# A fused state-space kernel: the second image of pair i + 2 scaled on VectorE instead of GpSimd, and the first cycle's scatters placed ahead of the scaling

## The chip, the cores and the metric

The kernel runs on one core of a Trainium2 chip. The metric is the device time of one execution in microseconds, as the median of three runs. A core has five engines that work side by side, each through its own queue in its own order: TensorE (PE in the profile) for matrix products, VectorE (DVE), ScalarE (ACT), GpSimd (POOL) and SyncE (SP), which here only starts DMA transfers. They meet at semaphores: an instruction waits until a counter has reached a number, and another one raises it. Matrix products land in PSUM, everything else stands in SBUF or in DRAM.

## The reference

The input x has 16 images of 256 channels and 32 x 32 points. Two residual blocks follow each other:

```
x = x + L0(group_norm(x))     # gate: softmax; experts: relu; x * sigmoid(scale per image and channel)
x = x + L1(group_norm(x))     # below, per image, N = 1024 tokens
  xz  = silu(in_proj_w @ x + in_proj_b);  x_ssm, res, gate = split(xz, 3)
  xf  = silu(conv1d(x_ssm, 3 taps, per channel) + dw_b)
  dbc = dbc_w @ xf + dbc_b;  dt, B, C per head (2 heads, 8 states)
  xf, dt, B, C reordered along the tokens by a permutation per head
  h_t = exp(dt_t * A) * h_{t-1} + dt_t * B_t * x_t;   y_t = C_t . h_t + D * x_t
  y   = y in the old order;  y = y * silu(gate) + res
  out = silu(out_proj_w @ y + out_proj_b)
```

L0 and both norms come down to one factor and one summand per image and channel. The kernel works these out from statistics of x and applies them to x once; this is the scaling that the change is about: x becomes x * P + B per channel, in place.

## The kernel before

The 16 images are worked in eight pairs. Three buffers `xb0` to `xb2` hold the pairs in turn, pair i in buffer i mod 3; each pair has two images (b = 0, 1) of two tiles of 128 channels x 1024 tokens. A loop of eight cycles runs on every engine, and cycle i of an engine holds work of three pairs: the recurrence, the gate, the residual and the output of pair i, the scattering of pair i + 1, and the scaling, the projection and the convolution of pair i + 2. Nothing plans the order: on each engine it is the order in which the functions `cycle(i)` are written, and each instruction waits for the one in front of it on its engine.

GpSimd does three things per cycle. `scale_x(i + 2, ...)` (L443, two instructions per image, one per tile) scales the images. `scatter(i + 1)` (L462) issues 16 indirect DMAs, which write the rows of `stage` into the DRAM tensor `xt_scratch` at the places that the permutation gives. `gather(i, h)` (L476) issues eight indirect DMAs per head, which bring the rows of the result back from `yt_scratch` into `crow`. `scattered` waits until all scatters have landed. Every wait of GpSimd goes through `hold`, which waits for a semaphore and counts on. In the order before, one image is scaled ahead of the scatters and the other behind them. `scale_x` waits for `pcur_ready` in front of its loop over the images:

```
if i < NB:
    hold(scales_ready, 1)
else:
    hold(pcur_ready, i + 1)
par = i % XB
for b in images:
    hold(x_in[par][b], x_loads(i))
```

`pcur_ready` is raised by VectorE when the parameters of a pair are in `pcur`: twice before the loop, then once for each later pair by `take_params` (L1027). In cycle 0 this stands late, after the parameters of pairs 2 to 7 have been worked out; in the later cycles it is VectorE's first instruction. The scatters need the bias on the rows in `stage`, which VectorE adds early in the cycle (L1046), and they need the loads of the pair before out of `xt_scratch` to be over.

TensorE begins the projection of pair i + 2 (L1429, 16 matmuls per image) behind the last matmuls of pair i's recurrence; image 0 comes first and then image 1, and each waits for its own count of scaled images. Behind them stand 24 matmuls of the residual, the turning back of the gathered rows (L1547), and the output (L1557). ScalarE empties PSUM; its results pass through VectorE's convolution (L1040). VectorE's carried states (L1120, L1122) end the recurrence of a cycle, and the convolution follows directly behind them. VectorE's last work on an image (L1225) adds the output to x; SyncE then stores the image, and loads an image of the pair three later into the same buffer.

Of the kernel before, what the change touches and what calls it, by code (L numbers as in the profile page):

```python
# [19 lines left out]
ALU = mybir.AluOpType  # L20
# [6 lines left out]
CT = C // P  # L27
H, S = 2, 8
E, R = 8, 16
NB = 2  # L30
# [37 lines left out]
PRM_P, PRM_S, PRM_B, PRM_BIAS, PRM_W = 0, 2, 4, 6, 12  # L68
# [30 lines left out]
def build(nc, x_d, w1g_d, b1g_d, w2_d, b2_d, inw_d, inb_d, dww_d, dwb_d, dbcw_d, dbcb_d, alog_d,  # L99
          alogt_d, dpar_d, mob_d, outw_d, outb_d, const_d, out_d):  # L100
    with ExitStack() as ctx:
        def sb(name, width, dt=F32):
            return ctx.enter_context(nc.sbuf_tensor(name, [P, width], dt))

        def sem(name):
            return ctx.enter_context(nc.semaphore(name))

        def v(tensor, off, *dims, parts=P, p0=0):

            width = tensor.shape[1]  # L110
            assert off + sum(step * (count - 1) for step, count in dims) < width
            return bass.AP(tensor, p0 * width + off, [[width, parts]] + [list(d) for d in dims])
# [8 lines left out]
        XB = 3  # L121
# [27 lines left out]
        pcur = sb("pcur", XB * NB * PRM_W)  # L149
# [39 lines left out]
        x_in = [[sem(f"x_in{par}{b}") for b in range(NB)] for par in range(XB)]  # L189
# [29 lines left out]
        ranks_ready = sem("ranks_ready")  # L219
        pcur_ready = sem("pcur_ready")  # L220
        x_scaled = sem("x_scaled")
        a_full, a_drained = sem("a_full"), sem("a_drained")
        g_full, g_drained = sem("g_full"), sem("g_drained")
        e_full, e_drained = sem("e_full"), sem("e_drained")
# [48 lines left out]
        def first(i):  # L273
            return isinstance(i, int) and i == 0
# [11 lines left out]
        def x_loads(i):  # L286

            return 16 * (1 + i // XB)
# [19 lines left out]
        def x_view(par, b, ct, off=0, n=N):  # L308
            return v(xb[par], (b * CT + ct) * N + off, (1, n))
# [113 lines left out]
        def _(pool):  # L423

            def hold(semaphore, value):

                if isinstance(value, int) and value <= 0:
                    return
                pool.wait_ge(semaphore, value)
                pool.sem_inc(pool_passed, 1)  # L430

            def scale_x(i, images=range(NB)):
# [8 lines that stand above are left out]
                    params = v(pcur, (par * NB + b) * PRM_W, (1, PRM_W))  # L441
                    for ct in range(CT):
                        last = nc.gpsimd.tensor_scalar(x_view(par, b, ct), x_view(par, b, ct),  # L443
                                                       params[:, PRM_P + ct:PRM_P + ct + 1],
                                                       params[:, PRM_B + ct:PRM_B + ct + 1], ALU.mult, ALU.add)
                    last.then_inc(x_scaled, 1)

            def scatter(i):
                for nt in range(NT):

                    if nt % BIAS_TILES == 0:

                        hold(stage_ready, i * BIAS_U + 2 + nt // BIAS_TILES)
                    if nt == 0:

                        hold(dbc_rows_in, 16 * (1 + H) * i)
                        for h in range(H):
                            hold(x_rows_in[h], 16 * i)
                        hold(c_stored, 16 * i)
                    for h in range(H):  # L460
                        k = h * NT + nt
                        pool.indirect_dma_start(  # L462
                            out=xt_d.ap(), out_offset=bass.IndirectOffsetOnAxis(ap=idx[:, k:k + 1], axis=0),
                            in_=v(stage, (nt * H + h) * ROW, (1, ROW)), in_offset=None).then_inc(rows_scattered, 16)

            def scattered(i):
                hold(rows_scattered, 256 * (i + 1))
# [13 lines left out]
                    hold(y_gathered[1], 128 * (i + 1))  # L481

            def cycle(i):
                if i < PH - 2:
                    scale_x(i + 2, (0,))
                if i < PH - 1:
                    scatter(i + 1)
                if i < PH - 2:
                    scale_x(i + 2, (1,))
                if i < PH - 1:  # L490
                    scattered(i + 1)
                for h in range(H):
                    gather(i, h)
# [317 lines left out]
        def _(dve):  # L811
# [207 lines left out]
            def take_params(i):  # L1019

                if i == NB:
                    dve.wait_ge(params_ready, 1)
                if i >= XB:

                    dve.wait_ge(out_ready, (i - XB + 1) * NB * CT)
                    dve.wait_ge(e_drained, (i - XB + 1) * E_U)
                nc.vector.tensor_copy(v(pcur, i % XB * NB * PRM_W, (1, NB * PRM_W)),  # L1027
                                      v(prm, i * NB * PRM_W, (1, NB * PRM_W))).then_inc(pcur_ready, 1)

            def convolve(i, b, tiles=range(CT)):  # L1030

                for ot in tiles:
                    step = (i * NB + b) * 3
                    dst = v(xf[b], ot * N, (1, N))
                    tap = lambda k: v(xs, ot * (N + 2) + k, (1, N))
                    wt = lambda k: v(small, DWW + ot * 3 + k, (1, 1))
                    for k in (1, 2):

                        dve.wait_ge(conv_step[ot], step + k)
                        nc.vector.scalar_tensor_tensor(dst, tap(k), wt(k), dst, ALU.mult, ALU.add).then_inc(conv_step[ot], 1)  # L1040
# [187 lines left out]
            def cycle(i):  # L1228
                more, beyond = i < PH - 1, i < PH - 2
                if beyond and not first(i):  # L1230
                    take_params(i + 2)
                if first(i):
                    turned_factors(i, 0)
                    scan(i, 0, 0)
                    token_products(i, 0)

                    token_weights(i, 0)
                    weights_block(i, 0)
                    scan(i, 0, 1)
                else:  # L1240
                    scan(i, 0, 0)
                    token_weights(i, 0)
                if more:
                    add_bias(i + 1, 0, 0, NT)
                    add_bias(i + 1, 1, 0, BIAS_TILES)
                if not first(i):
                    scan(i, 0, 1)
                if more:
                    add_bias(i + 1, 1, BIAS_TILES, BIAS_TILES)
                if not first(i):  # L1250
                    weights_block(i, 0)
                carried(i, 0)
                factors(i, 1)
                if first(i):
                    rescaled(1)
                token_products(i, 1)
                scan(i, 1, 0)
                if first(i):
                    turned_factors(i, 1)
                    group_variance(1, P_SUMS2, V_VAR2)  # L1260
                    token_weights(i, 1)
                    scaled(1)
                else:
                    token_weights(i, 1)
                    turned_factors(i, 1)
                weights_block(i, 1)
                scan(i, 1, 1)
                if first(i):
                    biases(1, 0, 3 * CT, P_BIAS2, params_ready)
                    take_params(i + 2)  # L1270
                carried(i, 1)
                if beyond:
                    for b in range(NB):
                        convolve(i + 2, b)
                if more:
                    softplus(i + 1)
                for b in range(NB):
                    gated(i, 0, b)
                    add_residual(i, 0, b)
                for b in range(NB):  # L1280
                    gated(i, 1, b)
                    add_residual(i, 1, b)
                if more:
                    factors(i + 1, 0)
                output(i, i % XB, 0)
                if more:
                    turned_factors(i + 1, 0)
                    token_products(i + 1, 0)
                output(i, i % XB, 1)
# [54 lines left out]
        def _(pe):  # L1344
# [88 lines left out]
            def project(i, b, before):  # L1433

                if first(i) and b == 0:
                    pe.wait_ge(x_first, 2)
                else:
                    pe.wait_ge(x_scaled, i * NB + b)
                for k in range(4):
                    o = pj_slot(k, a_drained, i * A_U + b * 4, before)  # L1440
                    part(o, i % XB, b, 0, k // 2, k % 2).then_inc(a_full, 1)
# [275 lines left out]
```

## Time and profile before

| | |
|---|---|
| median of 3 runs | 838.59 us (837.87 to 839.11) |
| the profiled execution | 842.28 us, span 840.5 us |
| PE busy | 735.4 us, 88% |
| DVE busy | 592.7 us, 71% |
| ACT busy | 508.6 us, 61% |
| POOL busy | 354.4 us, 42% |
| chain that ended last | POOL 28%, PE 20%, DMA 19%, DVE 15%, issue 13% |

The span runs from the first instruction to the last; the execution's own time is 1.8 us longer. Busy shares are means over stages with different limits: cycle 0 and the last cycles are not like cycles 1 to 5. The chain is followed back from the last instruction, at each step to what released it; "issue" in it is time for which the profile shows no wait. The rows below have start and duration in microseconds from the span's start, and in brackets the idle time of the engine ahead of the row with what ended it.

### The profile page before, as it was taken

How to read it: one execution, taken by the hardware profiler on the slowest of the kernel's cores; microseconds unless marked ns; L12 is line 12 of the kernel's file. 1: busy time of each engine (PE TensorE's matmuls, PEld its weight loads, DVE VectorE, ACT ScalarE, POOL GpSimd, SP SyncE). 2: the span in 40 equal slices, each digit the busy share in tenths (PEclk: the TensorE clock that was granted, in tenths of full speed). 3: DMA queues.
4: the chain of work that ended last, by engine and by line, in shares of the span. 5: the costliest groups of instructions: out<-in, count | busy, mean ns of one | idle time of the engine just before them, and what ended most of it. 6: DMA issues, size and time to landing. Idle time of an engine off the chain costs nothing.

```text
span 840.5 us, 11680 instructions
## 1 busy us (share of the span) xinstructions
PE 735.4 (88%) x4190; PEld 435.9 (52%) x4190; DVE 592.7 (71%) x1097; ACT 508.6 (61%) x954; POOL 354.4 (42%) x325
## 2 busy tenths in 40 slices
PE   2599867929999999999999999999999999697976
PEld 1356556614566456545755565546654566354642
DVE  5699589624787578957894779577957786378533
ACT  5775745426764875488467756676667764544422
POOL 2295300377038711873087407760577037600330
PEclk9699857969999999999999999999999999998989
DMA  9924550248464937484747564765568434942332
GB/s 329 369 101 165 143 128 1 83 134 212 107 213 144 245 87 246 136 215 120 219 143 189 164 183 156 190 194 131 195 191 213 115 131 142 254 114 87 110 92 100
DMA packets 128539, 136.40 MB, mean 162 GB/s; under 512 B 57305, under 2 KB 107106, under 8 KB 126434
## 3 DMA queue, kind: packets, MB, share of 16 engines
q1 hardware_dynamic: 114448, 99.42, 41.3%
q0 software_dynamic: 12288, 35.80, 13.1%
q10 hardware_dynamic: 1746, 0.45, 0.3%
q8 instruction: 33, 0.54, 0.3%
q14 instruction: 24, 0.20, 0.1%
HBM read 83.08 MB, written 53.61 MB: 163 GB/s over the span
## 4 chain that ended last, share of the span: by engine, by line
POOL 28%; PE 20%; DMA 19%; DVE 15%; issue 13%; ACT 4%; SPq 0%; POOLq 0%; DVEq 0%; ACTq 0%
POOL xt_scratch L462 15%; POOL crow L476 11%; DMA out<-xb 7%; PE pj L1557 7%; PE pj L1429 5%; DMA xb<-in_x 3%; DMA crow<-yt_scratch,idx 3%; DMA xt_scratch<-stage,idx 3%; DVE xf L1040 2%; DVE rs L894 2%; PE tp L1547 2%; POOL xb L443 2%; DMA crow<-cd_scratch 1%; PE tp L1449 1%; DVE xb L1225 1%
## 5 line engine op out<-in xcount | busy, mean ns | idle before, releaser
L1429 PE MATMUL pj<-xb,inw 128*128 128x512 f32 x768 | 350.4, 608 | 21.5 <-POOL xb L443 16.0
L1429 PEld LDWEIGHTS pj<-xb,inw 128*128 128x128 f32 x768 | 144.7, 194 | 187.2 <-issue 155.9
L462 POOL DMA_INDIRECT xt_scratch<-stage,idx x128 | 152.0, 1188 | 80.9 <-issue 73.7
L476 POOL DMA_INDIRECT crow<-yt_scratch,idx x128 | 135.0, 1054 | 109.5 <-DMA yt_scratch<-rs 62.1
L443 POOL TENSOR_SCALAR xb<-xb,pcur 128x1024 f32<-128x1024 f32 x30 | 46.5, 1559 | 257.2 <-DMA xb<-in_x 170.3
L1040 DVE SCALAR_TENSOR_TENSOR xf<-xs,small,xf 128x1024 f32<-128x1024 f32 x64 | 83.9, 1322 | 76.0 <-ACT xf L634 74.5
L1557 PE MATMUL pj<-gt,outw 128*128 128x512 f32 x256 | 118.9, 596 | 0.1
L734 ACT ACTIVATE rs<-pj,small 128x512 f32<-128x512 f32 x64 | 44.2, 694 | 58.1 <-PE pj L1557 58.0
L677 ACT COPY stage<-tp 128x256 f32<-128x256 f32 x128 | 47.8, 374 | 44.9 <-PE tp L1451 42.1
L690 ACT COPY rs<-pj 128x512 f32<-128x512 f32 x64 | 33.0, 600 | 67.7 <-PE pj L1524 67.7
L703 ACT ACTIVATE gt<-pj,pcur 128x512 f32<-128x512 f32 x64 | 41.5, 687 | 46.0 <-PE pj L1429 45.9
L1449 PE MATMUL tp<-dw,xf 128*128 128x162 f32 x256 | 63.3, 331 | 4.8 <-ACT stage L678 3.9
L1557 PEld LDWEIGHTS pj<-gt,outw 128*128 128x128 f32 x256 | 46.6, 192 | 38.2 <-issue 37.4
L1225 DVE SCALAR_TENSOR_TENSOR xb<-xb,pcur,rs 128x1024 f32<-128x1024 f32 x32 | 41.0, 1284 | 35.2 <-ACT rs L734 35.2
L1449 PEld LDWEIGHTS tp<-dw,xf 128*128 128x128 f32 x256 | 46.5, 204 | 36.5 <-issue 26.8
L627 ACT ACTIVATE xs<-pj,pcur 128x512 f32<-128x512 f32 x64 | 41.7, 688 | 37.5 <-PE pj L1429 30.3
L1169 DVE TENSOR_TENSOR big<-big,crow 128x1024 f32<-128x1024 f32 x32 | 60.6, 1938 | 1.1 <-DMA crow<-cd_scratch 1.0
L1451 PE MATMUL tp<-dw,xf 128*128 128x162 f32 x256 | 59.6, 317 | 0.0
L1212 DVE TENSOR_TENSOR gt<-tp,gt 128x512 f32<-128x512 f32 x64 | 41.2, 683 | 25.9 <-PE tp L1547 25.8
L724 ACT ACTIVATE rs<-pj,pcur 128x512 f32<-128x512 f32 x56 | 36.1, 687 | 28.9 <-PE pj L1429 24.7
L1547 PE MATMUL tp<-dw,crow 128*128 128x128 f32 x256 | 36.9, 286 | 15.9 <-DMA crow<-yt_scratch,idx 13.0
L665 ACT ACTIVATE big<-sg,small 128x272 f32<-128x272 f32 x128 | 50.1, 502 | 0.2
(256 smaller groups left out, 1059.0 us busy)
## 6 DMA issues: line engine op xcount, KB each, us to landing
xb<-in_x SPq DMA_DIRECT2D x16, 1024.0 KB, 5.7
xp<-xt_scratch SPq DMA_DIRECT2D x16, 1024.0 KB, 9.6
crow<-cd_scratch SPq DMA_DIRECT2D x16, 1024.0 KB
out<-xb SPq DMA_DIRECT2D x16, 1024.0 KB, 6.4
yt_scratch<-rs SPq DMA_DIRECT2D x16, 512.0 KB, 3.6
yt_scratch<-rs SPq DMA_DIRECT2D x32, 256.0 KB, 5.4
gt<-in_x SPq DMA_DIRECT2D x4, 1024.0 KB, 12.0
big<-in_x SPq DMA_DIRECT2D x4, 1024.0 KB, 13.7
```

Of the source, the lines that this page charges most:

```text
L443: last = nc.gpsimd.tensor_scalar(x_view(par, b, ct), x_view(par, b, ct), params[:, PRM_P + ct:PRM_P + ct + 1], params[:, PRM_B + ct:PRM_B ...
L462: pool.indirect_dma_start(out=xt_d.ap(), out_offset=bass.IndirectOffsetOnAxis(ap=idx[:, k:k + 1], axis=0), in_=v(stage, (nt * H + h) * ROW ...
L476: pool.indirect_dma_start(out=v(crow, k * NB * P, (1, NB * P)), out_offset=None, in_=yt_d.ap()[0:(h + 1) * N], in_offset=bass.IndirectOffs ...
L665: last = nc.scalar.activation(v(big, s * EEW, (1, EEW)), v(sg, 0, (1, EEW)), ACT.Exp, scale=v(small, ANEG + h * S + s, (1, 1)))
L1040: nc.vector.scalar_tensor_tensor(dst, tap(k), wt(k), dst, ALU.mult, ALU.add).then_inc(conv_step[ot], 1)
L1169: nc.vector.tensor_tensor(v(big, W_OFF + b * NT * L, (Q * L, S), (L, NT), (1, L)), v(big, SEG + b * NT * L, (EEW, S), (L, NT), (1, L)), v( ...
L1225: nc.vector.scalar_tensor_tensor(x_view(par, b, ot), x_view(par, b, ot), std, v(rs, (b * CT + ot) * N, (1, N)), ALU.mult, ALU.add).then_in ...
L1429: last = nc.tensor.matmul(o[:, :], v(inw, ct * 3 * C + col + ot * P, (1, P)), x_view(par, b, ct, nt * HALF, HALF), start=(ct == 0), stop=( ...
L1449: nc.tensor.matmul(v(o, 0, (1, P + HK)), tile(0), v(dw, HK, (1, P + HK)), start=True, stop=False, skip_group_check=True)
L1451: nc.tensor.matmul(v(o, P, (1, HK + P)), tile(1), v(dw, 0, (1, HK + P)), start=False, stop=True, skip_group_check=True).then_inc(x_full, 1)
L1547: last = nc.tensor.transpose(v(o, e * P, (1, P)), v(crow, (h * NT + nq * 4 + e) * NB * P + b * P, (1, P)), const("ident"))
L1557: last = nc.tensor.matmul(o[:, :], v(outw, h * C + ot * P, (1, P)), v(gt, (b * CT + h) * N + nt * HALF, (1, HALF)), start=(h == 0), stop=( ...
```

## The change

VectorE gets a `scale_x` of its own, and in cycles 0 to 5 scales image 1 of pair i + 2 behind the carried states of the second head, with two instructions and a semaphore of its own, `x_scaled_v`. GpSimd scales image 0 alone. In cycle 0 GpSimd calls `scale_x` with an empty list ahead of the scatters and scales image 0 behind them; in the later cycles it scales image 0 ahead of the scatters, and the call behind them has the empty list. TensorE waits for image 0 of the later pairs on `x_scaled`, with new counts, and for image 1 on `x_scaled_v`.

```diff
             def cycle(i):
+
+                early = 1 if i else 0
                 if i < PH - 2:
-                    scale_x(i + 2, (0,))
+                    scale_x(i + 2, range(0, early))
                 if i < PH - 1:
                     scatter(i + 1)
                 if i < PH - 2:
-                    scale_x(i + 2, (1,))
+                    scale_x(i + 2, range(early, 1))
                 if i < PH - 1:
                     scattered(i + 1)
...
+            def scale_x(i, b):
+
+                par = i % XB
+                dve.wait_ge(pcur_ready, i + 1)
+                dve.wait_ge(x_in[par][b], x_loads(i))
+                params = v(pcur, (par * NB + b) * PRM_W, (1, PRM_W))
+                for ct in range(CT):
+                    last = nc.vector.tensor_scalar(x_view(par, b, ct), x_view(par, b, ct), params[:, PRM_P + ct:PRM_P + ct + 1],
+                                                   params[:, PRM_B + ct:PRM_B + ct + 1], ALU.mult, ALU.add)
+                last.then_inc(x_scaled_v, 1)
...
                 carried(i, 1)
                 if beyond:
+                    scale_x(i + 2, 1)
                     for b in range(NB):
                         convolve(i + 2, b)
...
                 if first(i) and b == 0:
                     pe.wait_ge(x_first, 2)
+                elif i < NB:
+                    pe.wait_ge(x_scaled, i * NB + b)
+                elif b:
+                    pe.wait_ge(x_scaled_v, i - 1)
                 else:
-                    pe.wait_ge(x_scaled, i * NB + b)
+                    pe.wait_ge(x_scaled, 2 + i)
```

GpSimd's queue in cycle 0, from the end of pair 0's scatters to the gathers, before the change (a row is an instruction with its waits; `x_in20` and `x_in21` are the loads of images 0 and 1 into buffer 2):

```order
L443 TENSOR_SCALAR xb2<-xb2,pcur 128x1024 [waits rows_scattered,pcur_ready,x_in20]
L443 TENSOR_SCALAR xb2<-xb2,pcur 128x1024
L462 DMA xt_scratch<-stage,idx 2048x290 [waits stage_ready,dbc_rows_in,x_rows_in0,x_rows_in1,c_stored]
L462 DMA xt_scratch<-stage,idx 2048x290 x7
L462 DMA xt_scratch<-stage,idx 2048x290 [waits stage_ready]
L462 DMA xt_scratch<-stage,idx 2048x290 x7
L443 TENSOR_SCALAR xb2<-xb2,pcur 128x1024 [waits pcur_ready,x_in21]
L443 TENSOR_SCALAR xb2<-xb2,pcur 128x1024
L476 DMA crow<-yt_scratch,idx 128x256 [waits rows_scattered,y_stored0,w_ready]
```

The same place of GpSimd's queue after the change (lines have moved by one):

```order
L463 DMA xt_scratch<-stage,idx 2048x290 [waits rows_scattered,pcur_ready,stage_ready,dbc_rows_in,x_rows_in0,x_rows_in1,c_stored]
L463 DMA xt_scratch<-stage,idx 2048x290 x7
L463 DMA xt_scratch<-stage,idx 2048x290 [waits stage_ready]
L463 DMA xt_scratch<-stage,idx 2048x290 x7
L444 TENSOR_SCALAR xb2<-xb2,pcur 128x1024 [waits pcur_ready,x_in20]
L444 TENSOR_SCALAR xb2<-xb2,pcur 128x1024
L477 DMA crow<-yt_scratch,idx 128x256 [waits rows_scattered,y_stored0,w_ready]
```

The scaling of image 0 has moved behind the 16 scatters, the scaling of image 1 is gone, and the first scatter now carries the wait for `pcur_ready`.

VectorE's queue in cycle 0, around the end of the carried states of the second head, after the change (`hs1` are its states, `xf0` and `xf1` the convolved images):

```order
L1030 COPY pcur<-prm 128x24 [waits params_ready]
L1134 COPY hs1<-st 128x128 [waits carry_full]
L1136 SCALAR_TENSOR_TENSOR hs1<-st,dcy,hs1 128x128 x7
L1040 TENSOR_SCALAR xb2<-xb2,pcur 128x1024 [waits x_in21,pcur_ready]
L1040 TENSOR_SCALAR xb2<-xb2,pcur 128x1024
L1054 SCALAR_TENSOR_TENSOR xf0<-xs,small,xf0 128x1024 [waits conv_step0] x2
L1054 SCALAR_TENSOR_TENSOR xf0<-xs,small,xf0 128x1024 [waits conv_step1] x2
```

Two instructions stand between the carried states and the convolution that were not there; cycles 1 to 5 have the same two at the same place.

## Rows read from the trace of the kernel before

**Rows 1.** Chain of waits in cycle 2: start, duration (us), what.
```profile
315.69 11.82 DMA out<-xb
...
360.07 4.15 DMA xt_scratch<-stage,idx
...
402.33 1.30 DVE xb L1225
```

**Rows 2.** Timeline of TensorE, cycle 0: start, duration, instruction, count [idle before <-releaser].
```profile
164.73 7.13 PE L1429 MATMUL pj<-xb,inw 128*128 128x512 f32 x16
187.81 19.79 PE L1429 MATMUL pj<-xb,inw 128*128 128x512 f32 x40 [15.95 <-POOL xb L443]
```

**Rows 3.** Windows of cycle 0: stretch, its length, busy us, PEclk, DMA share, GB/s.
```profile
164.70:172.00 7.30, 7.16 (x18) 2.97 (x16) 0.00 (x0) 7.27 (x10) 5.71 (x6) 1.00 0.70 200
...
177.00:187.80 10.80, 0.00 (x0) 0.00 (x0) 0.28 (x1) 0.00 (x0) 7.17 (x7) 0.50 0.23 83
187.80:191.10 3.30, 3.29 (x4) 1.52 (x5) 0.00 (x0) 0.00 (x0) 2.57 (x3) 0.50 0.86 108
```

**Rows 4.** Timeline of TensorE in cycle 2.
```profile
358.65 24.30 PE L1429 MATMUL pj<-xb,inw 128*128 128x512 f32 x56
...
388.96 1.09 PE L1547 MATMUL tp<-dw,crow 128*128 128x128 f32 x8 [0.82 <-DMA crow<-yt_scratch,idx]
```

**Rows 5.** Timeline of GpSimd in cycle 0.
```profile
159.66 2.37 POOL L443 TENSOR_SCALAR xb<-xb,pcur 128x1024 f32<-128x1024 f32 x2 [67.07 <-DVE pcur L1027]
162.19 1.01 POOL L462 DMA_INDIRECT xt_scratch<-stage,idx  x1 [0.16 <-issue]
...
172.35 1.92 POOL L462 DMA_INDIRECT xt_scratch<-stage,idx  x1 [0.30 <-issue]
...
180.60 0.97 POOL L462 DMA_INDIRECT xt_scratch<-stage,idx  x1 [2.48 <-issue]
...
185.40 2.36 POOL L443 TENSOR_SCALAR xb<-xb,pcur 128x1024 f32<-128x1024 f32 x2
```

**Rows 6.** Timeline of VectorE in cycle 0.
```profile
134.29 0.86 DVE L1046 TENSOR_TENSOR stage<-stage,small 128x272 f32<-128x272 f32 x3
...
159.16 0.18 DVE L1027 COPY pcur<-prm 128x24 f32<-128x24 f32 x1
...
161.69 1.89 DVE L1122 SCALAR_TENSOR_TENSOR hs<-st,dcy,hs 128x128 f32<-128x128 f32 x7
172.15 5.12 DVE L1040 SCALAR_TENSOR_TENSOR xf<-xs,small,xf 128x1024 f32<-128x1024 f32 x4 [8.57 <-ACT xf L634]
```

**Rows 7.** Timeline of GpSimd in cycle 2.
```profile
341.02 3.67 POOL L462 DMA_INDIRECT xt_scratch<-stage,idx  x1 [0.30 <-issue]
...
357.55 0.96 POOL L462 DMA_INDIRECT xt_scratch<-stage,idx  x1 [0.30 <-issue]
...
361.07 2.36 POOL L443 TENSOR_SCALAR xb<-xb,pcur 128x1024 f32<-128x1024 f32 x2
365.22 1.00 POOL L476 DMA_INDIRECT crow<-yt_scratch,idx  x1 [1.79 <-DMA xt_scratch<-stage,idx]
```

**Rows 8.** Timeline of VectorE in cycle 2.
```profile
340.00 3.84 DVE L1169 TENSOR_TENSOR big<-big,crow 128x1024 f32<-128x1024 f32 x2
...
355.61 1.89 DVE L1122 SCALAR_TENSOR_TENSOR hs<-st,dcy,hs 128x128 f32<-128x128 f32 x7
366.02 7.78 DVE L1040 SCALAR_TENSOR_TENSOR xf<-xs,small,xf 128x1024 f32<-128x1024 f32 x6 [8.52 <-ACT xf L634]
```

**Rows 9.** Timeline of VectorE in the setup.
```profile
35.61 0.81 DVE L1308 TENSOR_SCALAR xb<-xb,pcur 128x1024 f32<-128x1024 f32 x1
```

**Rows 10.** Timeline of GpSimd at the same place.
```profile
35.89 1.61 POOL L443 TENSOR_SCALAR xb<-xb,pcur 128x1024 f32<-128x1024 f32 x1 [19.58 <-DVE pcur L995]
```

**Rows 11.** Instructions on the images, 310 to 410: SyncE's loads, landing times.
```profile
L320 SPq DMA_DIRECT2D xb<-in_x x2: 379/380/380, 327.5 to 330.4; - x2
...
DMA to landing us min/median/max: 5.0/5.5/12.1
```

More of the change, by code:

```diff
@@ L221, in build @@
         x_scaled = sem("x_scaled")
+        x_scaled_v = sem("x_scaled_v")
         a_full, a_drained = sem("a_full"), sem("a_drained")
```

## The prediction

> **What bounds the kernel now.** I read the chain of waits first. In cycles 1 to 5 it runs in a ring: from the finished first image of a pair through its store, the load of a new image into the same buffer, GpSimd's scaling of it, GpSimd's 16 scatters and their landing, the 16 gathers, and TensorE's output back to VectorE. In the cycle shown the store starts at 315.69 and the next first image is finished at 403.63, so one ring takes 87.9 us [rows 1]. TensorE runs beside it with little to spare: it works without a gap from 358.65 to 382.95 [rows 4], and the turning back of the second head then waits 0.82 us for the gather. So GpSimd's queue is the bound of these five cycles, by 0.8 us, and what delays its scatters or gathers delays everything.
>
> The first cycle (cycle 0) is different. The timeline of TensorE there shows a hole: 16 matmuls of the projection of pair 2 (its first image) end at 171.86, and the other 40 (second image, then the residual) start at 187.81, after 15.95 us of waiting for GpSimd's scaling [rows 2]. The granted clock falls to 0.50 in the hole and is still there after it [rows 3]. So 40 matmuls take 19.79 us, where 56 take 24.30 in a later cycle [rows 2, 4]: at that pace 40 would take 17.36, and the fall costs 2.4 us.
>
> GpSimd's own timeline says why [rows 5]: it scales image 0 from 159.66 to 162.03, issues 16 scatters from 162.19 to 185.4, and scales image 1 from 185.40 to 187.77. It starts at 159.66 because VectorE's copy of pair 2's parameters ends at 159.34 [rows 6].
>
> **The first cycle after the change.** The scatters now stand ahead of the only scaling left on GpSimd, and VectorE scales image 1 behind the carried states. Two things follow, and the first is decided by a wait. The function that scales is still called with an empty list of images, and it waits for the parameters before it looks at the list. The program order shows that: the first scatter's wait names the parameters. So the scatters can't go at 135.2, when their last bias is added [rows 6], but only once the copy has ended at 159.34. GpSimd's first action on that wait came at 159.66 before; with the scatter's other waits in between I put the first scatter at 160.2 (159.7 to 160.5), 2.0 us earlier than before, which is all that leaving out image 0 in front gives.
>
> From there, the 16 scatters took 23.2 us before. In that stand one of 1.92 us, where a plain one takes 0.96, while a convolution ran on VectorE [rows 5, 6, 7], and an idle time of 2.48 us where 0.30 is usual and for which the profile names nothing [rows 5]. The convolution now comes later (it needs the projection): minus 1.0. VectorE's new scaling falls beside the scatters: plus 1.4 (worked out below). Of the idle time's surplus of 2.2 I count half, since nothing says whether it comes again: minus 1.1. That gives 22.5 us, so the scatters end at 182.7. The scaling of image 0 (2.37, rows 5) ends at 185.1. TensorE, which before began pair 2's projection at 164.73, waits for exactly this image first, since it takes image 0 before image 1. Image 1, ready on VectorE at about 165, helps nothing.
>
> From 185.1 TensorE has all 56 matmuls ahead: 24.3, plus the same 2.4 for the clock after a hole that is now 20 us long. They end at 211.8; before it was 187.81 + 19.79 = 207.6. **First term: +4.2.** Lower bound: scatters from 159.7, no idle surplus, no stall (23.2 - 1.0 - 2.2 = 20.0), so 182.1 and 208.8: +1.2. Upper bound: scatters from 160.5, idle time and convolution stall kept and the scaling's stall added (24.6), so 187.5 and 214.2: +6.6. The gathers start after the scaling at about 185 to 187; before, they stood behind a scaling that ended at 187.77. They stay hidden behind TensorE. On SyncE's queue the copy and the loads of the scattered rows wait for the scatters' landing, which comes some 2 us earlier; nothing waits for that.
>
> **Cycles 1 to 5.** GpSimd loses the scaling of image 1 (361.07 to 363.43), but after it the engine sat idle 1.79 us until the last scatter had landed, and only then started the gathers [rows 7]. The landing ends that wait, 4.15 us after the last issue [rows 1], so taking the scaling away gives nothing: 0. TensorE's wait moves to VectorE's semaphore: VectorE finishes image 1 at about 359, and TensorE needs it 16 matmuls after 358.65, near 365.6; before, GpSimd had it ready at 363.43. Gain 0. The load of image 1 was issued at 330.4 and lands in 5 to 12 us, so VectorE does not wait for it at 357.5, nor does the convolution queued behind it [rows 11]. VectorE itself is idle for 8.52 us there [rows 8], so two operations of 0.81 us [rows 9] are covered.
>
> What they cost may stand on GpSimd. A scatter's issue of 3.67 us ends at 344.69, 0.85 us after the pair of VectorE products that ran from 340.00 to 343.84 [rows 7, 8]: GpSimd's issue was held until both were over. That pair reads two tensors from SBUF. The new operation reads one, and the carried states, with one of two in PSUM, hold nothing up: the issues beside them take 0.96. The trace has one case of the new operation: at 35.61 VectorE's scaling of 0.81 us runs to 36.42, and GpSimd's scaling, begun at 35.89, takes 1.61 us in place of 1.18 [rows 9, 10], so it was held. VectorE's new pair starts at 357.50, when the carried states end [rows 8], and the 14th scatter is issued at 357.55 [rows 7]. If it is held until 357.50 + 1.62 = 359.12 and ends 0.85 later, it ends at 359.97 in place of 358.51: +1.46, which is the upper bound. The lower one is 0, if an issue isn't held by such an operation. Below 0 nothing can come, as the landing is not earlier. I take 1.2, near the upper bound: the nearest row shows a hold, two operations that follow at once overlap by some 0.1, and some of the delay may be lost in the landing. The alignment of carried states and 14th scatter is the same in all five cycles, since the hold before at 340 to 344 sets it anew. **Second term: 5 x 1.2 = +6.0.**
>
> The Trainium skill, "SBUF — State Buffer", section "Who interferes with whom", says that VectorE's tensor_scalar can run in a mode that takes the port pair shared with GpSimd for the whole instruction, and that whoever comes second is blocked; by it the second term would be the full 5 x 1.46 = 7.3, and GpSimd's 1.61 us [rows 10] agrees with it. The same section infers that a product of two SBUF tensors does not stall the writing of descriptors; the 3.67 us [rows 7] speak against that here, and by that inference alone the trace's holds would be unexplained.
>
> **Sum.** 4.2 + 6.0 = 10.2. The profiled execution took 842.28 us (span 840.5), so its like would take 852.5. It lies 3.7 above the median of the runs, 838.59, which gives 848.8.
>
> **Rivals.** (a) The hold does not bite: VectorE waits for GpSimd instead, or scatters are not held by a one-input operation. Then only the first term is left: 842.8. For it: no scatter in the trace is seen held by such an operation; against it: GpSimd's own scaling was [rows 10]. (b) Faster: the first cycle's scatters go out as soon as the last bias is added, at 135.2, as the words on the change have it. They end by about 161, GpSimd's scaling of image 0 by 163.5, before TensorE's 164.73, image 1 is ready at 165, and the hole goes with the clock's fall: 15.95 + 2.4 = 18.4 less, with the second term 838.59 - 18.4 + 6.0 = 826. It decides from the point where the first scatter starts before about 142. Against it stands the parameters' wait in the order; for it, the words alone. (c) The first cycle comes out near its lower bound and the hold does not bite: about 839.8, no change that can be told.
>
> **How the numbers follow.** Both terms: 0.62. Rival (a): 0.25. Rival (b): 0.05. Rival (c): 0.04. Beyond the sums (a second idle time of 2.5 us among the scatters, or landings that grow by more than the stall, each 5 times): 0.04. Forecast 848.8. The lowest sum is 838.59 + 1.2 = 839.8, the highest 838.59 + 6.6 + 7.3 = 852.5; with what the traces don't show above that, the range is 840 to 854. About 0.2% (1.7 us) is what a measurement can tell from no change. Faster is (b), 0.05; the same is (c) with a little of (a), 0.05; slower is the rest, 0.90.
>
> **What would show it.** In the profile after: the first scatter of cycle 0 near 160 and not 135; TensorE's hole from 164.7 to about 185, followed by 56 matmuls of about 26.7 us; the clock at 0.50 in it. In cycles 1 to 5: a scatter issue of some 2.2 us beside VectorE's scaling, a ring of about 89.1 us in place of 87.9, and idle GpSimd from the last scatter to the gathers. If the ring stays at 87.9, the second term is wrong; if TensorE's hole is gone, the first is.

## The result, and the profile after

The changed kernel takes 864.15 us (median of 4 runs, 856.62 to 865.39) against 838.45 for the kernel before on the same chip: ratio 1.029, 95% interval 1.025 to 1.033, so 21 to 28 us slower. The forecast was 848.8: the right sign, and 15.4 too low. A ratio leaves out runs that lie over 1.5% above the fastest of their kernel. The profiled execution has a span of 863.4 us and a mean granted clock of 0.917 (before 840.5 and 0.939): 22.9 more, and these are followed here.

The first cycle first. GpSimd's timeline of the kernel after (start, duration, instruction, count, [idle before <-releaser]):

```profile
161.94 0.96 POOL L463 DMA_INDIRECT xt_scratch<-stage,idx  x1 [67.25 <-issue]
...
164.47 1.28 POOL L463 DMA_INDIRECT xt_scratch<-stage,idx  x1 [0.31 <-issue]
166.06 1.13 POOL L463 DMA_INDIRECT xt_scratch<-stage,idx  x1 [0.30 <-issue]
...
179.68 0.97 POOL L463 DMA_INDIRECT xt_scratch<-stage,idx  x1 [2.35 <-issue]
...
184.50 2.37 POOL L444 TENSOR_SCALAR xb<-xb,pcur 128x1024 f32<-128x1024 f32 x2
```

And TensorE's, with the windows around it (stretch, length, busy us of PE, PEld, DVE, ACT, POOL, granted clock, DMA share, GB/s):

```profile
186.93 26.08 PE L1444 MATMUL pj<-xb,inw 128*128 128x512 f32 x56 [20.80 <-POOL xb L444]
```

```profile
165.00:187.00 22.00, 1.20 (x21) 1.01 (x17) 1.35 (x2) 5.84 (x8) 15.82 (x16) 0.61 0.46 144
187.00:190.50 3.50, 3.50 (x4) 1.44 (x5) 0.00 (x0) 0.00 (x0) 2.85 (x3) 0.50 0.90 112
190.50:213.00 22.50, 22.50 (x55) 10.01 (x54) 12.70 (x21) 17.01 (x22) 16.11 (x14) 1.00 0.67 189
```

The scatters don't start before the parameters are there: the copy of them ends at 160.67 in this trace, whose setup ran 1.3 us later than that of before. Why it did is not shown: 0.8 of it stands there at the first copy of parameters (36.26 against 35.43), long before cycle 0, but the copy ends at 160.48 to 160.89 in the other runs with the same first cycle (e1, e3 and e5 below) and at 158.18 to 159.71 in those with the old one (e2, e4 and e6). 16 scatters take 22.5 us, image 0 is scaled behind them, and TensorE stands still for 20.80 us in place of 15.95 [rows 2], then has all 56 matmuls ahead of it; the first 3.6 us of them fall into the stretch at 0.50.

The chain of waits in the later cycles (start, duration, what):

```profile
231.78 1.30 DVE xb L1239
233.10 11.22 DMA out<-xb
...
322.37 11.79 DMA out<-xb
...
367.32 5.65 DMA xt_scratch<-stage,idx
...
506.74 9.88 DMA out<-xb
```

One ring took 87.9 [rows 1]. The first is now 89.27 (233.10 to 322.37), and the next two are 184.37 together, 92.2 each; the two after them are as long (92.26 and 92.31 between finished first images). The landing of the last scatter takes 5.65 where it took 4.15 [rows 1]. In cycle 2 GpSimd and VectorE show where this begins; against [rows 7] and [rows 8]:

```profile
364.22 1.53 POOL L463 DMA_INDIRECT xt_scratch<-stage,idx  x1 [0.30 <-issue]
...
367.32 0.96 POOL L463 DMA_INDIRECT xt_scratch<-stage,idx  x1 [0.30 <-issue]
373.97 0.99 POOL L477 DMA_INDIRECT crow<-yt_scratch,idx  x1 [5.69 <-DMA xt_scratch<-stage,idx]
```

```profile
362.29 1.89 DVE L1136 SCALAR_TENSOR_TENSOR hs<-st,dcy,hs 128x128 f32<-128x128 f32 x7
364.10 1.53 DVE L1040 TENSOR_SCALAR xb<-xb,pcur 128x1024 f32<-128x1024 f32 x2
```

The 14th scatter, 0.96 before, takes 1.53 and ends at 365.75, 0.12 after VectorE's two scalings (365.63). The gathers then start 5.69 after the last scatter's issue; before, the scaling of 2.36 and the 1.79 of waiting made that 4.2. The queues tell why the landing grew: SyncE's queue (q1) carries the store of the second head's rows (yt_scratch). Its packets (count, MB, share of the DMA engines) between the packets of the 15th and of the 16th scatter, in the 1.5 us from 361.0 before and in the 3.0 us from 368.0 after:

```profile
q1 hardware_dynamic: 761, 0.39, 87.5%
```

```profile
q1 hardware_dynamic: 1439, 0.73, 89.0%
```

The last scatter, 0.57 us later against the carried states, finds nearly twice as many of the store's packets ahead of its own.

What makes 89.3 into 92.2 is in TensorE's timeline of cycle 2, where the wait for the second head's gather was 0.82 [rows 4]:

```profile
396.92 1.09 PE L1566 MATMUL tp<-dw,crow 128*128 128x128 f32 x8 [2.10 <-DMA crow<-yt_scratch,idx]
398.43 1.72 PE L1566 MATMUL tp<-dw,crow 128*128 128x128 f32 x8 [0.42 <-DVE gt L1226]
...
402.07 3.62 PE L1576 MATMUL pj<-gt,outw 128*128 128x512 f32 x4
...
406.08 1.88 PE L1576 MATMUL pj<-gt,outw 128*128 128x512 f32 x4
```

After the wait of 2.10 the same four output matmuls take 3.62 and, a moment later, 1.88. The windows of the first and the last of four such stretches, and of all the cycles, say it in the granted clock:

```profile
398.80:405.60 6.80, 6.80 (x20) 4.42 (x19) 4.09 (x7) 3.38 (x11) 0.00 (x0) 0.50 0.32 72
...
675.30:682.00 6.70, 6.70 (x20) 4.96 (x21) 4.36 (x7) 2.90 (x9) 0.00 (x0) 0.50 0.26 59
```

```profile
195.00:700.00 505.00, 484.14 (x2682) 282.31 (x2681) 369.68 (x600) 330.75 (x620) 217.89 (x180) 0.97 0.58 166
```

The same stretch of before stands at 1.00. So TensorE fell to the lower level (1.2 of 2.4 GHz) once in each of cycles 2 to 5, each time 1.5 to 1.8 us after the longer wait had ended. A fall costs 92.2 - 89.3 = 2.95 us, since turning back, sums and the first output matmuls are on the ring. In cycle 1 the wait was as long and no fall followed.

The account of the 22.9: setup 1.3 (cause not shown), first cycle 4.1 (first image finished at 233.08 in place of 227.65, less the 1.3), cycle 1 1.3, cycles 2 to 5 4 x 4.25 = 17.0, tail -0.7 (the difference to the span).

### The profile page after: what moved, and what is told of

Same layout as the page of the kernel before. It is cut to its first block, busy times and chain, and to the rows that moved or that the text cites. A ratio compares the mean times of both kernels' runs of the same rounds, so it can differ in the third digit from the quotient of the medians.

```text
span 863.4 us, 11680 instructions
## 1 busy us (share of the span) xinstructions
PE 750.2 (87%) x4190; PEld 445.5 (52%) x4190; DVE 601.4 (70%) x1109; ACT 509.9 (59%) x954; POOL 339.3 (39%) x313
## 4 chain that ended last, share of the span: by engine, by line
POOL 28%; PE 26%; DMA 17%; issue 12%; DVE 11%; ACT 5%; SPq 0%; POOLq 0%; DVEq 0%; ACTq 0%
POOL xt_scratch L463 15%; POOL crow L477 11%; PE pj L1576 9%; PE pj L1444 6%; DMA out<-xb 4%; DMA xb<-in_x 4%; DMA xt_scratch<-stage,idx 3%; DMA crow<-yt_scratch,idx 3%; PE tp L1468 2%; PE tp L1566 2%; PE tp L1470 2%; DVE xf L1054 2%; POOL xb L444 2%; DMA crow<-cd_scratch 1%; DVE xb L1239 1%
## 5 line engine op out<-in xcount | busy, mean ns | idle before, releaser
L463 POOL DMA_INDIRECT xt_scratch<-stage,idx x128 | 155.6, 1216 | 155.2 <-issue 143.7
L1576 PE MATMUL pj<-gt,outw 128*128 128x512 f32 x256 | 126.1, 626 | 0.1
L444 POOL TENSOR_SCALAR xb<-xb,pcur 128x1024 f32<-128x1024 f32 x18 | 29.1, 1624 | 202.5 <-DMA xb<-in_x 182.1
L1576 PEld LDWEIGHTS pj<-gt,outw 128*128 128x128 f32 x256 | 49.1, 201 | 41.6 <-issue 40.1
L1566 PE MATMUL tp<-dw,crow 128*128 128x128 f32 x256 | 39.8, 304 | 21.6 <-DMA crow<-yt_scratch,idx 18.6
L727 ACT ACTIVATE rs<-pj,pcur 128x512 f32<-128x512 f32 x56 | 36.1, 688 | 29.1 <-PE pj L1444 24.6
L1566 PEld LDWEIGHTS tp<-dw,crow 128*128 128x128 f32 x256 | 32.5, 154 | 39.5 <-DMA crow<-yt_scratch,idx 27.0
```

The lines of the kernel that those rows point to most:

```text
L463: pool.indirect_dma_start(out=xt_d.ap(), out_offset=bass.IndirectOffsetOnAxis(ap=idx[:, k:k + 1], axis=0), in_=v(stage, (nt * H + h) * ROW ...
L1566: last = nc.tensor.transpose(v(o, e * P, (1, P)), v(crow, (h * NT + nq * 4 + e) * NB * P + b * P, (1, P)), const("ident"))
L1576: last = nc.tensor.matmul(o[:, :], v(outw, h * C + ot * P, (1, P)), v(gt, (b * CT + h) * N + nt * HALF, (1, HALF)), start=(h == 0), stop=( ...
```

## The experiments

The theory to test: the first cycle costs its 4.1 by itself. In the later cycles VectorE's scaling holds the 14th scatter, the last landing slips behind more of the store, TensorE waits 2.1 in place of 0.8, and that wait, not anything of VectorE's work as such, lets the clock fall. Rivals: the clock falls because the first cycle shifted everything, or because VectorE scales at all, or the landing grows because GpSimd no longer scales there.

**e1: the first cycle alone.** In cycles 1 to 5 GpSimd scales both images again (i is the cycle; the same condition stands in VectorE's program, and TensorE waits for the engine that scales).

```diff
+BY_DVE = (0,)
...
-                    scale_x(i + 2, range(early, 1))
+                    scale_x(i + 2, range(early, 1 if i in BY_DVE else NB))
```

> Only the first cycle is as in the changed kernel (scatters ahead of GpSimd's scaling of image 0, VectorE scales image 1); in cycles 1 to 5 GpSimd scales both images as before. Theory (first term of the prediction, and the clock falls come from the later cycles' longer wait): +4.1 to +4.2 us on the kernel before's 838.45, so 842.6, the distance between finished first images 87.97 in every cycle, granted clock never at 0.5 between 200 and 720 us. Rival (the first cycle's new order moves all later work so that TensorE's clock falls in cycles 2 to 5): 842.6 + 4 x 2.95 = 854.4, with rings of about 90.9.

Measured 843.73 us (10 runs), ratio 1.005 (1.0025 to 1.0075): +4.2 (2.1 to 6.3). In the chain of waits all rings are 88.07, 88.01, 88.07, 88.07:

```profile
233.29 11.29 DMA out<-xb
321.36 11.91 DMA out<-xb
...
585.51 10.99 DMA out<-xb
```

The granted clock from 195 to 700 is 1.00. The first term stands by itself with its forecast size, and the first cycle's shift causes no fall.

**e2: the later cycles alone.** The first cycle is as before; VectorE scales image 1 in cycles 1 to 5.

```diff
+BY_DVE = (1, 2, 3, 4, 5)
...
-                early = 1 if i else 0
+                early = 1
...
-                    scale_x(i + 2, range(early, 1))
+                    scale_x(i + 2, range(early, 1 if i in BY_DVE else NB))
```

> The first cycle is as in the kernel before; VectorE scales the second image in cycles 1 to 5. Theory (the later cycles' delay of 1.3 us lengthens TensorE's wait for the second head's gather, and the granted clock falls to 0.5 behind it in cycles 2 to 5): 838.45 + 5 x 1.3 + 4 x 2.95 = 856.8, rings of 92.2 in cycles 2 to 5 and 0.5 granted for some 7 us in each. Rival (the falls need the first cycle's shift): 838.45 + 6.5 = 845.0, rings of 89.3.

Measured 852.65, 851.22, 857.24 and 844.26 us; ratio 1.010 (1.004 to 1.017) without the third. The profiled run (852.65) has rings of 89.28 and 89.26 in cycles 1 and 2, then 92.30, 92.20 and 92.17. TensorE at the turn-back of cycle 1 and of cycle 3:

```profile
301.13 1.09 PE L1568 MATMUL tp<-dw,crow 128*128 128x128 f32 x8 [2.09 <-DMA crow<-yt_scratch,idx]
302.64 1.25 PE L1568 MATMUL tp<-dw,crow 128*128 128x128 f32 x8 [0.41 <-DVE gt L1227]
...
479.72 1.09 PE L1568 MATMUL tp<-dw,crow 128*128 128x128 f32 x8 [2.13 <-DMA crow<-yt_scratch,idx]
481.23 1.71 PE L1568 MATMUL tp<-dw,crow 128*128 128x128 f32 x8 [0.42 <-DVE gt L1227]
```

The falls come without the first cycle's change. The wait is the same in both cycles and the clock falls behind one of them only: the wait makes a fall possible, not certain. The four times fit no fall (844.3, the 845.0 of the rival) to four (857.2, the 856.8 of the theory); only one of the runs has a trace, so the number of falls of the others is argued from their times.

**e3: the wait filled.** In cycles 1 to 5 TensorE runs four matmuls of 128x512 into a PSUM tile that nobody reads, ahead of its wait for the second head.

```diff
+                if h and 0 < i < PH - 2:
+                    o = tp_slot(4, y_drained, i * Y_U, before)
+                    for _ in range(4):
+                        nc.tensor.matmul(o[:, :], v(inw, 0, (1, P)), v(inw, 0, (1, HALF)), start=True, stop=True)
                 pe.wait_ge(y_gathered[h], 128 * (i + 1))
```

> The changed kernel with four added 128x512 matmuls on TensorE in cycles 1 to 5, just ahead of its wait for the second head's gather, into a PSUM tile that nobody reads; nothing else differs. Theory (the granted clock falls because TensorE stands still about 2.1 us there): the falls in cycles 2 to 5 go, rings of 89.3, 864.15 - 4 x 2.95 = 852.4. Rival (the falls have another cause, such as VectorE's scaling or the convolution's place): 0.5 granted as before, 864 or more, since the added matmuls can only take time.

Measured 858.12 us (857.24 to 860.56), ratio 1.023 (1.019 to 1.027). TensorE in cycle 2 (each of the four calls stands there twice), and the windows of all cycles:

```profile
396.16 3.60 PE L1564 MATMUL tp<-inw 128*128 128x512 f32 x8
399.60 1.04 PE L1570 MATMUL tp<-dw,crow 128*128 128x128 f32 x8
401.05 1.25 PE L1570 MATMUL tp<-dw,crow 128*128 128x128 f32 x8 [0.42 <-DVE gt L1226]
```

```profile
195.00:700.00 505.00, 494.80 (x2770) 286.87 (x2768) 376.33 (x607) 332.83 (x631) 214.97 (x180) 1.00 0.58 168
```

The falls are gone, though VectorE scales as in the changed kernel and the gathers start as late (5.5 us behind the last scatter in four of the five cycles). The time expected was missed by 5.7, because the filling lasts 3.60, longer than the wait that it covers: it adds 1.1 to each ring (90.35 to 90.44 in place of 89.27), 5.6 in all. The rival expected 0.5 as before, and the stretch stands at 1.00: that is its end. The time leans the same way (858.1 in place of 864.2 with twenty added matmuls), but the intervals of the two ratios, 1.019 to 1.027 and 1.025 to 1.033, overlap, so it doesn't decide by itself.

**e4: a delay without VectorE.** The kernel before, with five small memsets on GpSimd between the landing and the gathers of cycles 1 to 5, each waiting for the one ahead.

```diff
                     scattered(i + 1)
+                if 0 < i < PH - 2:
+                    for k in range(5):
+                        nc.gpsimd.memset(idle[:, :], 0.0).then_inc(idled, 1)
+                        nc.gpsimd.wait_ge(idled, (i - 1) * 5 + k + 1)
```

> The kernel before (GpSimd scales both images) with five small memsets of 128x200 on GpSimd, each waiting for the one ahead, between its wait for the scatters and the gathers in cycles 1 to 5: some 1.3 to 2 us of delay of the gathers and no VectorE scaling. Theory (a later gather alone tips the clock): 838.45 + 5 x 1.3 (to 2) + 4 x 2.95 = 857 to 861, 0.5 granted in cycles 2 to 5. Rival (VectorE's scaling is needed for the falls): 838.45 + 6.5 to 10 = 845 to 848, granted clock 1.0 there.

Measured 839.28, 853.98, 846.59 and 846.71 us; ratio 1.012 (1.006 to 1.017) without the second. In the profiled run (839.28) TensorE at the turn-back of cycle 1 and of cycle 3:

```profile
302.11 1.09 PE L1553 MATMUL tp<-dw,crow 128*128 128x128 f32 x8 [2.10 <-DMA crow<-yt_scratch,idx]
303.62 1.25 PE L1553 MATMUL tp<-dw,crow 128*128 128x128 f32 x8 [0.42 <-DVE gt L1218]
...
478.74 3.51 PE L1553 MATMUL tp<-dw,crow 128*128 128x128 f32 x16 [2.19 <-DMA crow<-yt_scratch,idx]
```

The rings are 89.23, 87.33, 90.31, 89.30 and 87.33. In cycle 3 a wait of 2.19 is followed by a short fall, with a ring 1.0 longer than those of cycles 1 and 4. So a fall needs no scaling on VectorE. This rests on one fall in one trace: the waits of 2.10 in cycle 1 and of 2.18 in cycle 4 had none, and the times miss the 857 to 861 of the theory, while two of the four lie in the rival's 845 to 848. The run is weaker than it was meant to be: in cycles 2 and 5 the scatters themselves were faster (22.97 and 23.80 in place of some 24.6; in cycle 2 two issues of 1.77 and 1.57 stand beside VectorE's long products in place of one of 3.67 [rows 7]), TensorE waited for no gather, and its own 87.33 set the ring.

**e5: the scaling late.** The changed kernel, but VectorE's scaling of cycles 1 to 5 waits until GpSimd has issued its last scatter.

```diff
                     scale_x(i + 2, range(early, 1))
+                    nc.gpsimd.memset(v(mark, i, (1, 1)), 0.0).then_inc(issued, 1)
...
                 dve.wait_ge(x_in[par][b], x_loads(i))
+                if i > NB:
+                    dve.wait_ge(issued, i - 1)
```

> The changed kernel, but in cycles 1 to 5 VectorE's scaling waits until GpSimd has issued its last scatter of the cycle (a one-element memset behind it raises a semaphore). Theory (VectorE's two scalings at the 14th scatter hold GpSimd by 0.57 us, that puts the last scatter's packets behind the store of the second head, and all of the later cycles' loss follows from it): scatters back to 24.4 us, gathers 4.1 us or less behind the last scatter, rings of 87.97, no 0.5 granted in cycles 2 to 5, so 842.6 with the first cycle's 4.2. Rival (the landing grows because GpSimd no longer scales image 1 there, wherever VectorE does it): gathers still some 5.4 behind the last scatter, rings of 88.5 to 89, and the clock may fall: 845 to 858.

Measured 844.70 us (10 runs), ratio 1.006 (1.0035 to 1.008): +4.9 (2.9 to 6.9), what the first cycle alone costs. The chain and VectorE in cycle 2:

```profile
320.90 11.14 DMA out<-xb
...
365.37 4.12 DMA xt_scratch<-stage,idx
...
408.88 11.78 DMA out<-xb
```

```profile
366.59 1.53 DVE L1045 TENSOR_SCALAR xb<-xb,pcur 128x1024 f32<-128x1024 f32 x2 [3.88 <-POOL mark L495]
```

The rings are 87.98, the landing 4.12, the clock from 195 to 700 stands at 1.00. VectorE does the same work 3.9 us later against the carried states, GpSimd still doesn't scale, and the later cycles' whole loss is gone. This takes the last rival away: the landing grew by the hold of the 14th scatter.

**e6: image 0 in front of the first cycle's scatters.** GpSimd scales image 0 where it did before, VectorE image 1, and the later cycles are as before.

```diff
+BY_DVE = (0,)
...
-                early = 1 if i else 0
+                early = 1
...
-                    scale_x(i + 2, range(early, 1))
+                    scale_x(i + 2, range(early, 1 if i in BY_DVE else NB))
```

> First cycle: GpSimd scales image 0 ahead of the scatters, as before, and VectorE scales image 1, so GpSimd's 2.36 us scaling of image 1 is gone from behind the scatters; cycles 1 to 5 as in the kernel before. Theory (in the first cycle TensorE waited for image 1's scaling behind the 16 scatters, 16 of its 56 matmuls and the clock's 0.5 hung on it): the wait to 185 goes to that of the first head's gather at about 208, TensorE's projection runs from 165, so at most some 18 us off: 820; at least the matmuls leave the stretch behind the scatters. Rival (the gathers of the first cycle, which start at 187.9 and end at 209.3, bound it, and they stay): nothing gained, 838 to 840.

Measured 839.06 us (10 runs), ratio 1.000 (0.998 to 1.0025). My expectation failed. TensorE:

```profile
165.05 24.30 PE L1446 MATMUL pj<-xb,inw 128*128 128x512 f32 x56
204.44 1.97 PE L1568 MATMUL tp<-dw,crow 128*128 128x128 f32 x8 [15.09 <-DMA crow<-yt_scratch,idx]
```

The hole goes from in front of the second image to behind the projection, 15.09 us with its fall of the clock, since the gathers start no earlier than before, at 189.72. In this order the first cycle hangs on the chain scatters, landing, gathers, and taking image 1 from behind the scatters only shifts where TensorE waits for it. In the changed kernel the end of TensorE's 56 matmuls decides: it comes at 213.0 in place of 207.6, and the first finished image is as much later, while the gathers start at 187.04, no later than before (187.92).

**e7: the first cycle's scatters truly early.** As e1, and the function that scales does nothing at all for an empty list.

```diff
             def scale_x(i, images=range(NB)):
+                if not len(images):
+                    return
                 if i < NB:
```

> As the first cycle of the changed kernel and cycles 1 to 5 of the kernel before, but with the call on no image taken out whole, so that the first cycle's 16 scatters don't wait for the current parameters (pcur) and go as soon as their rows are there, near 135. Theory (that empty call's wait is what kept the scatters at 162): scatters 135 to 158, image 0's scaling at 160, gathers up to 25 us earlier, 820 (842.6 less some 22). Rival (the rows that the scatters carry are themselves late, or the setup's other DMAs fill the queue): scatters at 155 or later, 835 to 842.

Measured 821.09 us (818.06 to 821.75), ratio 0.9785 (0.975 to 0.982): 15 to 21 us faster than before. GpSimd and TensorE in the first cycle:

```profile
135.61 0.96 POOL L466 DMA_INDIRECT xt_scratch<-stage,idx  x1 [42.77 <-DVE stage L1063]
...
162.51 2.36 POOL L447 TENSOR_SCALAR xb<-xb,pcur 128x1024 f32<-128x1024 f32 x2
165.21 1.08 POOL L480 DMA_INDIRECT crow<-yt_scratch,idx  x1 [0.34 <-issue]
```

```profile
165.81 24.29 PE L1448 MATMUL pj<-xb,inw 128*128 128x512 f32 x56
189.93 1.04 PE L1570 MATMUL tp<-dw,crow 128*128 128x128 f32 x8
```

The scatters go as soon as their last bias is added, the gathers start at 165.2, and TensorE has no hole. The wait of the empty call costs 843.73 - 821.09 = 22.6 against e1, or some 22 by the two ratios to the kernel before, since e1 and e7 ran on different chips.

**e8: the changed kernel with e7's two lines.**

> The changed kernel with the call on no image taken out whole: first cycle's scatters near 135, VectorE scales image 1 in all cycles. Theory: the first cycle gives some 22 us back, rings stay 89.3 without and 92.2 with a clock fall: 842 with four falls, 830 with none. Rival (the falls come from the first cycle's late start alone): rings of 88, 824.

Measured 835.77 us (9 runs, 826.02 to 847.47), ratio 0.992 (0.988 to 0.996) without the two longest. The profiled run (837.24) has rings of 89.22 and 89.23, and from cycle 3 on 92.32, 92.23 and 92.23, with a fall of the clock in each; the windows of the first and the last:

```profile
466.90:473.70 6.80, 6.80 (x19) 4.41 (x18) 4.01 (x7) 3.34 (x10) 0.00 (x0) 0.50 0.30 73
...
651.20:658.00 6.80, 6.80 (x20) 4.61 (x19) 4.23 (x7) 3.25 (x10) 0.00 (x0) 0.50 0.30 72
```

Some 21 us of the first cycle come back (its first image is finished at 211.85 in place of 233.08), and the later cycles keep their loss, which rules out that the falls came from the late first cycle. The runs differ by 21.5 us, more than the 14.8 of five falls; only one has a trace, and the kernel before, without falls in its cycles 1 to 5, differs by 6.7 in the same series.

**e9: e8 with e5's late scaling.**

> The changed kernel with both mendings: the call on no image taken out whole (first cycle's scatters near 135), and in cycles 1 to 5 VectorE's scaling waits for GpSimd's last scatter. Theory (the two causes add, and an image scaled on VectorE behind the scatters is neither gain nor loss): rings of 87.3 to 88.0, no 0.5 granted in cycles 2 to 5, 821 as with GpSimd scaling both images in cycles 1 to 5. Rival (the 2.36 us that GpSimd saves shows once the first cycle is early): below 818.

Measured 821.67 us (817.70 to 823.00), ratio 0.981 (0.977 to 0.985), rings of 87.99 to 88.13. The two causes add up, and these runs can tell no third: with both mended, an image scaled on VectorE is worth as much as one on GpSimd. Of all versions e7 and e9 are the fastest, and the same within what was measured.

## Why the prediction was right in its first term and wrong in its second

**The first cycle: right.** The forecast was +4.2; the trace gives 4.1 beside the setup's 1.3, and e1 4.2 (2.1 to 6.3), which holds both sums. The deciding point, that the empty call still waits for the parameters, is shown by e7. Inside the sum pieces were off and cancelled, so that it comes out so close is luck in part: the idle time among the scatters came in full (2.35, of whose surplus I had counted half), and VectorE's scaling held the scatters by 0.5 in place of 1.4. The scatters took the forecast 22.5. The first of them came 1.27 behind the copy in place of 0.86, and the 56 matmuls took 26.08 in place of 26.7.

**The later cycles, the delay: right in size, partly for another reason.** "I take 1.2": each ring without a fall is 1.3 longer. But I had the issue held by up to 1.46 and the landing unchanged. The 14th scatter was held by 0.57, the landing grew by 1.4, because the last scatter came behind more packets of the store, and the 16 gathers ran 0.7 faster (21.4 in place of 22.1 in the mean of five cycles), at a time when fewer of them stood beside VectorE's convolution: 0.57 + 1.4 - 0.7 = 1.3. The nearest row that I chose (two products, held until 0.85 behind their end) priced the hold too high; the issue went on 0.12 behind VectorE's end. The Trainium skill, "SBUF — State Buffer", section "A bandwidth-pool intuition that's wrong (but worth ruling out)", has a blocked GpSimd go on some 0.115 us behind VectorE's end; the trace agrees (0.12).

**The later cycles, the clock: the step that failed.** "Second term: 5 x 1.2 = +6.0" and its upper bound of 7.3 count a late gather as a delay that TensorE passes on one for one. The runs show that it doesn't end there: the wait of 2.1 us at the turn-back lets the granted clock fall to 0.50 for 6.8 us, on the ring, for 2.95 more. Four falls make 11.8, most of the 15.4 by which the forecast was too low; with the 1.3 of five rings the later cycles cost 18.3 in the profiled run in place of 6.0. (A further 2.7 of the 15.4 is that the profiled execution of before lay 3.7 above its median, that of after 1.0.) e3 (no standing still, no falls), e5 (no late gather, no falls), e2 and e8 (falls without the late first cycle) and e4 (a fall without VectorE's scaling) show it. I had the falls of the clock in my table for the first cycle's hole of 16 us [rows 3], and never asked what a wait of 2 us would do. The rows that I chose held no case: the one wait there is 0.82 [rows 4], without a fall. But the trace of before held one, outside the ring. TensorE in its cycle 6, and a window behind the first of these waits:

```profile
720.56 5.40 PE L1429 MATMUL pj<-xb,inw 128*128 128x512 f32 x8 [2.78 <-ACT rs L724]
...
736.36 1.09 PE L1547 MATMUL tp<-dw,crow 128*128 128x128 f32 x8 [2.90 <-DMA crow<-yt_scratch,idx]
```

```profile
721.80:725.00 3.20, 3.20 (x5) 1.19 (x4) 0.00 (x0) 0.59 (x1) 2.56 (x3) 0.50 1.13 177
```

After work nearly without a gap from 699.80 to 717.78, a wait of 2.78 is followed by a fall of 3.4 us, and eight matmuls take 5.40 where eight take 3.60 at the full clock; a wait of 2.90 a little later is followed by none. That was there to be read: a wait of this length may bring a fall or not, and the range could have held it.

**The rivals.** (a), no hold, is refuted by the 1.53 and by e5. (b), scatters at 135.2, didn't come with this change; e7, in which GpSimd scales in the later cycles, so that the second term isn't in it, shows that it was the right mechanism with the right price, 18.0 (15 to 21) against the 18.4 worked out. (c) is refuted with (a).

**What stays open.** What decides whether a wait of 2.1 us makes the clock fall. It didn't in cycle 1 of the changed kernel nor in cycles 1 and 2 of e2 and e8, nor in cycles 1 and 4 of e4, with waits of the same length. Once a fall had come in the changed kernel, e2 and e8, each later cycle up to 5 had one too; a ring with a fall lasts 92.2 and the falls follow each other at that distance. The shorter fall of e4 had none behind it. The runs don't tell why. Since e3 also lengthens the rings to 90.4, it may have shifted what this hangs on; but it has no fall in five cycles, and neither have e5 and e9, where the wait is back at 0.83 to 0.99. How many falls the runs without a trace had is argued from their times alone, and the setup's 1.3 is open too.

## What to carry to other kernels

Where TensorE waits inside a ring that it nearly fills, price a longer wait twice: by its length, and by the matmuls behind it at half the clock, and look for cases of the second in the whole trace, not only in the ring. A call with an empty list of work can still wait: look at what the first instruction behind it names. And when an engine takes over work "behind" another's, put it behind the whole of the queue that it can hold up, here behind the last scatter, where the same two instructions cost nothing.

## What the runs showed of the hardware

TensorE's granted clock fell behind a wait of 2.1 us in a stretch where it had been busy nearly without a gap (0.50 for 6.8 us), and in the kernel before behind one of 2.78 (0.50 for 3.4 us); waits of the same length without a fall stand beside both. A DMA issued by GpSimd can land 1.4 us later for being issued 0.57 later, when another queue's packets run in between: 1439 of them in place of 761. And an idle time of 2.35 to 2.9 us between the 12th and the 13th scatter of the first cycle came in all eleven traces, wherever the scatters start (162 or 135), without a releaser in the profile; no run here was made to find its cause.
